# Layer 1 of a two-layer graph network: a third group of 128 rows a turn picked by column copies, hotT made by tensor_scalar, steps of three engines re-ordered

## What is computed

```python
e_in = jnp.concatenate([x[src], x[dst]], axis=-1)
edge_new = _mlp(e_in, We1, be1, We2, be2)             # relu(h @ W1 + b1) @ W2 + b2
agg = jax.ops.segment_sum(edge_new, dst, num_segments=x.shape[0])
mesh_new = _mlp(jnp.concatenate([x, agg], axis=-1), Wn1, bn1, Wn2, bn2)
return x + mesh_new
```

## Time and profile before

| | |
|---|---|
| median of three runs | 4093.22 us |
| the profiled execution | 4090.99 us |
| its span, first to last instruction | 4088.8 us |
| first gather of layer 1 starts, last one starts | 2179.3 us, 4059.7 us |
| busy share of the span: TensorE, VectorE, ScalarE, GpSimd | 71%, 61%, 61%, 73% |

### The profile page before, as it was taken

How to read it: one execution, slowest core, us unless ns; L and a number is a source line. 1 busy time by engine, 2 the same in 40 slices (tenths; PEclk the granted TensorE clock), 3 DMA queues, 4 the chain that set the end, 5 groups by cost and what they waited for, 6 DMA issues and landing times. The chain is left out here.

```text
span 4088.8 us, 90253 instructions
## 1 busy us (share of the span) xinstructions
PE 2902.8 (71%) x18890; PEld 2648.6 (65%) x18891; DVE 2493.5 (61%) x5568; ACT 2497.4 (61%) x10068; POOL 2964.7 (73%) x3137
## 2 busy tenths in 40 slices
PE   6888888888888788888865565655556565666656
PEld 4877777777777777777744555555556555555656
DVE  4877777777777777777765444444444555555544
ACT  3767777777777677777646555455555555555553
POOL 5777777777777777777536777777777777777775
PEclk8999999999999999999987777767767777777777
DMA  6333333333333333333234333333333333333332
GB/s 190 81 81 81 83 81 81 81 82 81 82 80 82 81 84 81 81 81 83 57 108 108 95 90 94 94 91 94 90 94 94 93 99 94 98 97 95 97 99 63
DMA packets 426429, 367.97 MB, mean 90 GB/s; under 512 B 276875, under 2 KB 355163, under 8 KB 426108
## 3 DMA queue, kind: packets, MB, share of 16 engines
q0 software_dynamic: 98240, 214.20, 20.4%
q1 hardware_dynamic: 316720, 143.31, 14.0%
q10 hardware_dynamic: 11214, 8.17, 0.7%
HBM read 343.89 MB, written 21.44 MB: 89 GB/s over the span
## 5 line engine op out<-in xcount | busy, mean ns | idle before, releaser
L724 POOL DMA_INDIRECT he<-h_table,src_i x1563 | 1480.7, 947 | 514.9 <-issue 504.3
L1744 POOL DMA_INDIRECT msg<-p_table,src x1507 | 1422.3, 944 | 467.1 <-issue 461.6
L1777 PE MATMUL p_sumT<-msg,hot 128*80 128x129 f32 x3136 | 595.7, 369 | 688.2 <-ACT sumT L1830 683.7
L1777 PEld LDWEIGHTS p_sumT<-msg,hot 128*80 128x80 f32 x3136 | 542.5, 215 | 725.4 <-issue 533.9
L1622 ACT COPY picked<-hT 128x1 f32 x7168 | 759.9, 187 | 412.4 <-issue 398.3
L1762 PE MATMUL p_edge<-r_win,hotT 80*128 80x128 f32 x3136 | 480.0, 312 | 59.7 <-DVE msg L1899 45.8
L763 PE MATMUL p_score<-qk_two,heT 128*128 128x160 f32 x1568 | 396.7, 336 | 165.4 <-ACT heT L873 163.4
L1762 PEld LDWEIGHTS p_edge<-r_win,hotT 80*128 80x128 f32 x3136 | 452.6, 227 | 63.7 <-issue 63.2
L1899 DVE TENSOR_TENSOR msg<-msg,p_edge 128x512 f32<-128x512 f32 x392 | 243.6, 662 | 377.5 <-DMA msg<-p_table,src 376.4
L765 PE MATMUL p_score<-qk_win,heT 128*128 128x80 f32 x3136 | 465.2, 273 | 0.0
L765 PEld LDWEIGHTS p_score<-qk_win,heT 128*128 128x128 f32 x3136 | 454.3, 200 | 0.0
(11 more groups left out here) (210 smaller groups left out, 4565.5 us busy)
## 6 DMA issues: line engine op xcount, KB each, us to landing
dst_row<-in_dst_dram SPq DMA_DIRECT2D x196, 320.0 KB
feat<-in_edge_attr_dram SPq DMA_DIRECT2D x196, 128.0 KB
he<-h_table,src_i POOLq DMA_INDIRECT x1563
msg<-p_table,src POOLq DMA_INDIRECT x1507
qk_win<-qk_table SPq DMA_DIRECT2D x196, 40.0 KB
qk_two<-qk_table SPq DMA_DIRECT2D x392, 20.0 KB
r_win<-r_table SPq DMA_DIRECT2D x196, 40.0 KB
qk_table<-qk SPq DMA_DIRECT2D x13, 512.0 KB
```

Of the source, the lines that this page charges most:

```text
L724: e.indirect_dma_start(out=he[u][:, j, 2 * FE:2 * FE + ROW], out_offset=None, in_=h_table[:, :], in_offset=bass.IndirectOffsetOnAxis(ap=sr ...
L1744: e.indirect_dma_start(out=msg[u][:, j, 0:D], out_offset=None, in_=p_table[:, :], in_offset=bass.IndirectOffsetOnAxis(ap=src_i[u][:, j:j + ...
L1777: mm = e.matmul(p_sumT[:, :], hot_of(c)[:, j, :], msg[u][:, j, 0:D + 1], start=(j == 0), stop=(j == J - 1))
```

## The change

Three groups are picked a turn in place of two, of chunks 5, 0 and 3. ScalarE copies the columns of the first and the last, VectorE those of chunk 0. Chunks 0 and 3 of turn 0 are gathered whole, and `pick_first` is gone. Numbers are loaded into registers 16 at a time at most. hotT is made by `tensor_scalar`, which compares dst_row with `node_b` in SBUF (start plus number of the node, made once for all chunks). TensorE's step of chunk c is now edges of c + 1, turn_back of c - 1, sums of c; ScalarE's is copy_sums of c - 1, relu of c, columns; VectorE's is masks of c + 1, add of c - 2, columns, additions of c.

```diff
-PICKED = (5, 1)
-BATCH = 8
-BY_ACT = P // BATCH
+PICKED = (5, 0, 3)
+BY_ACT = (P, 0, P)
+BY_DVE = tuple(P - n for n in BY_ACT)
+AT_ONCE = 16
...
-                        return PICKED.index(c[1]) if at_first and c[1] in PICKED else None
+                        g = PICKED.index(c[1]) if at_first and c[1] in PICKED else None
+                        return None if g and isinstance(c[0], int) and c[0] == 0 else g
...
                     def pick_step(e, engine, copy, done, c, of):
-                        per = -(-len(PICKED) * of // SLOTS)
-                        at, end = c[1] * per, min((c[1] + 1) * per, len(PICKED) * of)
+                        per = -(-sum(of) // (SLOTS if of is BY_ACT else SLOTS - 2))
+                        at, end = c[1] * per, min((c[1] + 1) * per, sum(of))
...
                             i, u = c
-                            if u == 2 and not (isinstance(i, int) and i == 0):
+                            if u == 0 and not (isinstance(i, int) and i == 0):
+                                load_picks(2, i)
+                            elif u == 3 and not (isinstance(i, int) and i == 0):
                                 load_picks(0, i)
-                            elif u == 5 and not (isinstance(i, int) and i == TURNS - 1):
+                            elif u == 4 and not (isinstance(i, int) and i == TURNS - 1):
                                 load_picks(1, i + 1)
...
                         def step(c):
-                            if not is_first(c):
-                                sums(shift(c, -1))
-                            if not is_first(c) and not is_first(shift(c, -1)):
-                                turn_back(shift(c, -2))
                             if not is_last(c):
                                 edges(shift(c, 1))
+                            if not is_first(c):
+                                turn_back(shift(c, -1))
+                            sums(c)
...
-                        def step(c):
+                        def step(c, k=None):
+                            if not is_first(c):
+                                copy_sums(shift(c, -1))
+                            relus(c)
+                            if k is not None and c[1] == 4:
+                                relu_hidden(e, k)
                             if at_first:
                                 pick_step(e, mybir.EngineType.Activation, e.copy, picked_act, c, BY_ACT)
-                            if not is_first(c) and not is_first(shift(c, -1)):
-                                copy_sums(shift(c, -2))
-                            relus(c)
...
                             if j0:
-                                e.scalar_tensor_tensor(out=hotT_of(c)[:, 0, :], in0=dst_row[u][:, 0:P], scalar=start_b[0:W, bass.ds(number(c), 1)],
-                                                       in1=p_node.broadcast_to([W, P]), op0=ALU.subtract, op1=ALU.is_equal)
-                            e.scalar_tensor_tensor(out=hotT_of(c)[:, j0:J, :], in0=dst_row[u][:, j0 * P:CH].rearrange(row_j, j=J - j0),
-                                                   scalar=start_b[0:W, bass.ds(number(c), 1)], in1=p_node.unsqueeze(2).broadcast_to([W, J - j0, P]),
-                                                   op0=ALU.subtract, op1=ALU.is_equal).then_inc(hotT_done, 1)
+                                e.tensor_scalar(hotT_of(c)[:, 0, :], dst_row[u][:, 0:P], node_b[:, bass.ds(number(c), 1)], None, ALU.is_equal)
+                            e.tensor_scalar(hotT_of(c)[:, j0:J, :], dst_row[u][:, j0 * P:CH].rearrange(row_j, j=J - j0),
+                                            node_b[:, bass.ds(number(c), 1)], None, ALU.is_equal).then_inc(hotT_done, 1)
...
                                 hots(shift(c, 1))
-                            boths(c)
                             if not is_first(c) and not is_first(shift(c, -1)):
                                 add(shift(c, -2))
+                            if at_first:
+                                pick_step(e, mybir.EngineType.DVE, e.tensor_copy, picked_dve, c, BY_DVE)
+                            boths(c)
```

More of the change, by code:

```diff
@@ L1475, in gnn_kernel, with made @@
             picked_act = sem("picked_act")
-            def pick_number(g, turn):
-                return turn * len(PICKED) + (g - 1) % len(PICKED)
+            picked_dve = sem("picked_dve")
+            def made(of, g, turn):
+                each = sum(n > 0 for n in of)
+                upto = sum(n > 0 for n in of[0:g + 1])
+                return turn * each + (upto + each if g == 0 else upto)
             in_win_done = sem("in_win_done")
@@ L1615, in pick_columns @@
                                 e.sem_inc(passed, 1)
-                        for b in range(first, first + n):
-                            at = b * BATCH
+                        start = first + (0 if of is BY_ACT else BY_ACT[g])
+                        parts = -(-n // AT_ONCE)
+                        ends = [start + n * k // parts for k in range(parts + 1)]
+                        for at, to in zip(ends, ends[1:]):
                             _, nodes = nc.values_load_multi_w_load_instructions(
-                                picks_i[g][0:1, at:at + BATCH], engines=(engine,), min_val=0, max_val=N - 1,
+                                picks_i[g][0:1, at:to], engines=(engine,), min_val=0, max_val=N - 1,
@@ L1638, in pick_first @@
-                    def pick_first(e, engine, copy, done, of):
-                        pick_columns(e, engine, copy, done, 1, 0, 0, of, of)
+                        per = -(-sum(of) // (SLOTS if of is BY_ACT else SLOTS - 2))
+                        at, end = c[1] * per, min((c[1] + 1) * per, sum(of))
+                        for g in range(len(of)):
+                            low = sum(of[0:g])
+                            first, n = max(at - low, 0), min(end - low, of[g]) - max(at - low, 0)
+                            turn = c[0] if g == 0 else c[0] + 1
+                            if n > 0 and not (isinstance(turn, int) and turn == TURNS):
+                                pick_columns(e, engine, copy, done, g, turn, first, n, of)
@@ L1659, in load_picks @@
                             if not isinstance(turn, int) or turn > 0:
-                                before = val(e, pick_number(g, turn) - len(PICKED) + 1)
-                                e.wait_ge(picked_act, before)
-                                e.sem_inc(passed, 1)
+                                for done, of in ((picked_act, BY_ACT), (picked_dve, BY_DVE)):
+                                    if of[g]:
+                                        e.wait_ge(done, val(e, made(of, g, turn - 1)))
+                                        e.sem_inc(passed, 1)
                             at = val(e, (turn * SLOTS + PICKED[g]) * CH)
@@ L1713, in _ @@
                         if at_first:
-                            for g in (1, 0):
-                                load_picks(g, 0)
+                            load_picks(0, 0)
                         for u in range(1, SLOTS):
@@ L1763, in edges @@
                                     if j == 0 and g is not None:
-                                        ready = val(e, pick_number(g, c[0]) + 1)
-                                        e.wait_ge(picked_act, ready)
+                                        for done, of in ((picked_act, BY_ACT), (picked_dve, BY_DVE)):
+                                            if of[g]:
+                                                e.wait_ge(done, val(e, made(of, g, c[0])))
                                         mm = e.matmul(p_edge[0][:, 0, :], picked[g][:, :], we1[:, 0, :], start=False, stop=True)
@@ L1933, in step_grouped @@
                                 normal(e, k)
+                        e.tensor_scalar(node_b[:, :], start_b[0:W, :], node_c[:, 0:1], None, ALU.add).then_inc(fixed, 1)
+                        e.wait_ge(fixed, val(e, FIXED + 1 + r))
                         hots((0, 0))
                         if at_first:
+                            e.sem_inc(picked_dve, sum(n > 0 for n in BY_DVE))
                             e.sem_inc(y_done, 1)
```

41 lines of the change are left out of this document (17 added, 24 removed).

## The result

The changed kernel takes 4545.1 us, the median of four runs (4542.7 to 4547.4); the kernel before, run beside it, 4095.8. The ratio is 1.110 [1.108, 1.112]: slower by 449 us. The forecast was 4120, within 4053 to 4150. The profiled execution has a span of 4540.4 us, 451.6 more than before.

A forecast was written before the change was run, and what follows sets the result against it. The prediction took GpSimd's layer 1 gathers as the bound: 4091.0 - 32.5 (gathers) - 2.3 (tail) + 61.6 (hotT) = 4117.8, so 4120 us as median of runs, within 4053 to 4150.

The forecast's parts named there:

- GpSimd bounds, and a gather less is worth 1.249: Layer 1: GpSimd's gathers set the end, one per 1.249 us; 26 fewer gathers give -32.5 us.
- hotT keeps GpSimd out, + 61.6: Layer 1: hotT's new tensor_scalar delays gathers 0.55 us in each of 112 eight-row forms, +61.6 us, ends 12 and 103.
- the cap of 0.23: Longest gather wait shown by a row before; as a cap on hotT's blocking it makes the sum some 36 us lower.
- The tail, -2.3: End of the kernel: the last chunk's sums start right after its last relu, -2.3 us, bounds 0 and -3.
- Edits that I cost at nothing: ScalarE's column loads, VectorE's new columns and loads, and SyncE's extra loads in layer 1 were taken to add no time.
- 10 x 0.5: VectorE's ten loads of numbers a turn at 0.5 us each, part of about 17 us a turn for its new columns.
- 22 loads for 32: ScalarE's 256 columns a turn need 22 loads of numbers in place of 32, so fewer gaps and the same copies.
- 51 of 66 fits: VectorE's turn: about 17 us new work plus 33.5 old work, 51 us, fits in the 66 us a turn lasts.
- the cover of the seven tiles: Ring of seven message tiles: GpSimd needs a chunk's sums only seven chunks on, about 66 us, hiding some 7 us lateness.
- rival 3: VectorE becomes the bound: at 0.28 us a column its turn takes 74 us for 66; time 4274, chance 0.05.
- Rival 2: VectorE's column copies keep GpSimd out as well, 57 us more; time 4177, chance 0.12.
- Rival 1: hotT's tensor_scalar does not keep GpSimd out and the change does what it says; time 4058, chance 0.28.

The follow-up runs named there:

- second experiment: The change with all loads of numbers begun at multiples of four and hotT made as before: 4063.3 us, 0.992 of the kernel before.

## Why the prediction was wrong, point by point

**GpSimd bounds, and a gather less is worth 1.249: right, as long as nothing else bounds.** In the second experiment first to last gather took 4033.2 - 2185.4 = 1847.8 us for 1880.4: -32.6, where -32.5 was predicted.

**hotT keeps GpSimd out, + 61.6: right where GpSimd bounds.** 62.6 with the loads mended, 0.55 for each hotT, the value taken. The mechanism came out; that the value did to the hundredth is luck, since it was chosen between 0.23 and 0.68. In the change as it stands the price is hidden behind GpSimd's waits: with the old hotT the time is 4551.6 for 4545.1. One difference is small: 114 eight-row forms, not 112, since chunks 0 and 3 of turn 0 are whole. Two gathers beside hotT in the kernel after, in time order:

```profile
2610.11 1.17 DVE L1890 TENSOR_SCALAR hotT<-dst_row,node_b 80x1024 f32<-80x1024 int32 x1
2610.21 1.89 POOL L1753 DMA_INDIRECT msg<-p_table,src  x1 [0.30 <-issue]
...
3001.08 1.52 POOL L1753 DMA_INDIRECT msg<-p_table,src  x1 [0.30 <-issue]
...
3001.34 1.14 DVE L1890 TENSOR_SCALAR hotT<-dst_row,node_b 80x1024 f32<-80x1024 int32 x1
```

A gather that begins 0.10 after hotT lasts 0.95 longer than 0.944; one that is 0.26 under way when hotT begins ends 0.12 after it, 0.58 longer. hotT lasts 1.17 where about 1.1 was predicted. The mean distance of gathers with the loads mended is (4094.6 - 2184.2)/1480 = 1.291, predicted 1.29. The Trainium skill, SBUF — State Buffer, section "Who interferes with whom", which has the loser blocked for the whole instruction, agrees with the first of these rows; the cap of 0.23 that the prediction held against it came from shorter instructions. By the Trainium skill, VectorE: DVE Perf Modes, section "Mode 2×_2P", 1024 elements are 512 steps and seven rows don't qualify; the seven-row form took 1.83 us for 1.81 before and the eight-row form fell from 2.05 to 1.17, so the trace agrees on which goes two at a time. What steps of eight cost on top is shown by the last chunk's hotT, which is read without them, here with the loads mended:

```profile
4087.69 0.76 DVE L1890 TENSOR_SCALAR hotT<-dst_row,node_b 80x1024 f32<-80x1024 int32 x1
```

That is 0.4 us less than the 1.17 of the others.

**The tail, -2.3: right in size where the order stands alone**, -1.7, and the sums start 0.05 after the relu's end. It was -2.5 with the loads mended and + 1.6 with the old hotT besides; in the change it is + 44.4, since the whole pipeline is late.

**The step that failed is "Edits that I cost at nothing": the price of the loads of numbers.** With the loads mended the rest of the sum holds: + 26.8 by the prediction, + 29.2 measured; the loads cost the other 419 us. "10 x 0.5" for VectorE's turn is 6 x 2.95 + 2 x 1.1 + 2 x 0.86 = 21.6 us, and "22 loads for 32" on ScalarE, called fewer gaps, is 605 loads of 2.4 at the median for 896 of 0.55, in the whole layer. The 0.5 was read from loads of eight at multiples of eight and used for 12 and 13 from anywhere. Unlike the prices of a copy and of hotT, it was not bounded from both sides. The trace of before had a row for the upper side, loads of a single number:

```profile
L471 DVEq TENSOR_LOAD <-start_i x473: 297/304/699, 111.5 to 4069.4; - x158
```

13 x 0.30 is 3.9 us a load: 39 a turn on VectorE, and by the same row far over a turn's room on ScalarE. A page of the Trainium skill points the same way: Runtime: NRT & Kernel Launch, section "Instruction fetch mechanics", has about 200 ns for each register even in a bulk load; the loads that the page speaks of come from HBM, these from SBUF. The slow loads agree with it, 1.752/8 = 0.219 a number; the quick ones, 0.546/8 = 0.068, do not.

**"51 of 66 fits" failed with it, and once more.** With the measured loads VectorE's turn is 29 of other work and 37 of columns, 66: as a sum it would still just fit, and ScalarE's 72 would not. But the sum of an engine's work is not the bound where its instructions stand in a chain with other engines'. The prediction saw the place (columns ahead of the additions, with TensorE and ScalarE waiting behind), but priced it for chunk 0 alone, some 7 us once a turn, and saw nothing that uses up the cover of the seven tiles. The delay came in five steps of seven and used it up: 399.0 us of waits for sums.

**Rivals.** The outcome is rival 3's, compute takes over from GpSimd, which had a chance of 0.05; but its mechanism, dear copies, is not: VectorE's copies follow each other every 0.118 us (13 in 1.53), where 0.095 was predicted and rival 3 has 0.28. Rival 2 is wrong: with the loads mended every long gather but three lies beside hotT. Rival 1 is wrong of hotT; its 4058 is the time of another kernel, the one with the loads mended and the old hotT, 4063 measured.

## What to carry to other kernels

When a change alters how often or how many values are loaded into registers, take the load's price by its start as well as its count: here the same eight numbers cost 0.55 or 1.75 us by one address, and batches of 12 or 16 from multiples of four bring back 419 us. Bound every price that no row shows from both sides, the cheap-looking ones too, and price what stands between one engine's result and the next engine's start by the chain, not by the engine's share of busy time. An operation that is quicker on its own engine (2.05 to 1.17 us for hotT) can be the dearer one where it holds up the engine that bounds, 0.55 us each time.

## What the runs showed of the hardware that was not expected

- A load of numbers from SBUF into registers took 0.546 us for 8 and 0.79 for 12 on ScalarE, 0.86 for 12 and 1.10 for 13 on VectorE, where it began at a multiple of four numbers (16 bytes); 1.752 for 8, about 2.6 for 12 (ScalarE) and 2.95 for 13 (VectorE) elsewhere. That is about 0.07 and 0.22 us a number. From a multiple of four, 13 and 16 numbers (the latter the median with the loads mended) both took 1.10 on VectorE, 0.24 more than 12.
- An even start is not enough: VectorE's loads of 13 from 26 and 78 took 2.95.
- Slow work on two engines that stand in one loop added up, 199 + 220 for 419 in single runs, though either engine's own sum of work was at most a few us a turn over what GpSimd needs: the chain of a turn ran 51 us by VectorE and TensorE and then 30 by ScalarE.
